# Four value products of a head group issued in one run instead of one behind each of four transposed pairs

## The reference, cut to what matters

```python
xn = _layernorm(x, axis=-1)
# attention
q, k, v = split(xn @ w_attn)                        # 16 heads of 8
scores = einsum('bhqd,bhkd->bhqk', q, k) / sqrt(8) + causal - log1p(decay * log1p(dist))
y = einsum('bhqk,bhkd->bhqd', softmax(scores), v)
attn = y @ w_proj
# experts
gate = top-2 of softmax(xn @ Wr.T), normalised
ffn = sum_e gate_e * (silu(xn @ W1_e.T) @ W2_e.T)
out = x + attn + ffn
```

## Time and profile before

| | us |
|---|---|
| median of 3 runs | 603.96 |
| lowest and highest of them | 601.05, 605.42 |
| the profiled execution, whole | 606.9 |
| its span in the trace | 604.9 |
| slots 10 to 30, first transposed pair of slot 10 to that of slot 31 | 182.80 to 418.60 |

### The profile page before, as it was taken

The page is one execution under the profiler, slowest core; times in us unless marked ns, Lnnn a source line. Parts: engine busy times, 40 slices in busy tenths (PEclk is TensorE's granted clock), DMA queues, the critical chain, the costliest instruction groups (busy, mean ns, idle before and its releaser), DMA issues.

```text
span 604.9 us, 13661 instructions
## 1 busy us (share of the span) xinstructions
PE 524.3 (87%) x4443; PEld 372.9 (62%) x4443; DVE 357.6 (59%) x1430; ACT 320.7 (53%) x576; POOL 374.5 (62%) x610
## 2 busy tenths in 40 slices
PE   3554799978889999999999999999999999999940
PEld 1443555545545655655655655655689999999930
DVE  5524588768876676676777677676333333333326
ACT  3551576646667676676676676676633333233310
POOL 3212466635669889888689879889315455545534
PEclk9999999979989999999999999999999999999975
DMA  5322359046114224314214214306425766776539
GB/s 157 131 78 71 84 176 210 2 119 174 25 62 130 82 70 124 88 68 133 64 67 140 76 61 134 97 28 209 114 73 173 219 206 200 209 211 204 154 117 317
DMA packets 69715, 76.49 MB, mean 126 GB/s; under 512 B 8318, under 2 KB 52352, under 8 KB 69648
## 3 DMA queue, kind: packets, MB, share of 16 engines
q1 hardware_dynamic: 65328, 67.16, 38.3%
q0 software_dynamic: 4320, 8.47, 4.1%
HBM read 46.16 MB, written 29.89 MB: 126 GB/s over the span
## 4 chain that ended last, share of the span: by engine, by line
PE 70%; DVE 20%; ACT 3%; DMA 2%; issue 2%; POOL 1%; SPq 0%; DVEq 0%; POOLq 0%
PE psT L1163 18%; PE psO L1175 13%; PE ps L1209 11%; PE psT L1236 11%; DVE scores L1014 10%; PE ps L1141 6%; PE psM L1118 3%; PE psM L1083 2%; PE psM L1098 2%; PE psM L1193 1%; DVE x_all L479 1%; PE psM L1124 1%; DVE y L1031 1%; DVE xn_all L845 1%; PE ps L1200 1%
## 5 line engine op out<-in xcount | busy, mean ns | idle before, releaser
L1014 DVE CUSTOM_DVE_ANT_0 scores<-ps,wdist 128x256 f32<-128x256 f32 (+3 forms) x512 | 222.0, 486 | 114.4 <-PE ps L1141 113.3
L660 POOL TENSOR_SCALAR scores<-scores,row_max 128x384 f32<-128x384 f32 (+2 forms) x448 | 224.4, 516 | 85.8 <-DVE row_max L1014 84.7
L764 ACT ACTIVATE probs<-psT 128x512 f32<-128x512 f32 x320 | 173.9, 596 | 59.6 <-PE psT L1163 59.4
L1163 PE MATMUL psT<-ident,scores 128*128 128x128 f32 x1280 | 176.3, 281 | 4.7 <-ACT probs L764 3.8
L1163 PEld LDWEIGHTS psT<-ident,scores 128*128 128x128 f32 x1280 | 140.9, 143 | 44.2 <-issue 32.2
L678 POOL DMA_INDIRECT picked_dram<-scores,row_ring x71 | 69.8, 983 | 83.8 <-DVE scores L1058 82.4
L1175 PE MATMUL psO<-probs,values 128*32 128x512 f32 (+3 forms) x1024 | 96.6, 452 | 0.0
L782 ACT ACTIVATE scores<-ps 128x512 f32<-128x512 f32 x71 | 42.4, 597 | 93.9 <-PE ps L1209 93.9
L1236 PE MATMUL psT<-wdist,scores 128*128 x568 | 75.5, 276 | 0.7 <-issue 0.4
L1209 PE MATMUL ps<-scores,wdist 128*128 128x128 f32 x568 | 75.1, 275 | 0.7 <-DVE scores L1046 0.7
L671 POOL DMA_INDIRECT rows_dram<-xn_all x64 | 62.8, 981 | 16.2 <-issue 16.2
(11 more groups left out here) (133 smaller groups left out, 356.1 us busy)
## 6 DMA issues: line engine op xcount, KB each, us to landing
wdist<-w1t SPq DMA_DIRECT2D x71, 256.0 KB, 3.3
k_rows<-k_dram SPq DMA_DIRECT2D x64, 96.0 KB, 2.9
q_rows<-q_dram SPq DMA_DIRECT2D x64, 96.0 KB, 2.5
row_ring<-rows_dram SPq DMA_DIRECT2D x71, 65.0 KB, 3.1
probs<-picked_dram SPq DMA_DIRECT2D x8, 512.0 KB, 7.3
rows_dram<-row_ring SPq DMA_DIRECT2D x7, 585.0 KB, 5.6
k_dram<-k_parts SPq DMA_DIRECT2D x8, 384.0 KB, 2.4
q_dram<-q_parts SPq DMA_DIRECT2D x8, 384.0 KB, 2.6
```

What stands on the lines that cost most here:

```text
L660: last = nc.gpsimd.tensor_scalar(part, part, -1.0, row_max[:, r, tile, quad:quad + 1], ALU.mult, ALU.add)
L764: nc.scalar.activation(probs[:, at.ring(2), w, :], psT[:, w % 2], ACT.Exp, scale=-1.0).then_inc(exp_ready, 1)
L1014: last = nc.vector.tensor_tensor_reduce(out=scores[:, r, u, col:col + n], in0=bank[:, col:col + n], in1=wdist[:, at.g * QUADS + quad, SEQ ...
L1163: last = nc.tensor.transpose(psT[:, w % 2, place * P:(place + 1) * P], scores[:, at.ring(2), u, col + key * P:col + (key + 1) * P], ident[:])
```

## The change

The three later value chunks move forward to directly behind the first. Nothing is added or removed. As ScalarE's copy of `psO` belongs to the fourth chunk, it moves with it.

```diff
     step("TE", n - 1, NGROUP, 0, 2)
     step("SA", n, NGROUP)
-    step("PV", n - 2, NGROUP, 0)
+    for chunk in range(TILES):
+        step("PV", n - 2, NGROUP, chunk)
     p1(1)
     per_batch("KR", -3)
     per_batch("QR", -2)
     step("TE", n - 1, NGROUP, 2, 4)
-    step("PV", n - 2, NGROUP, 1)
     per_batch("KM", -3)
...
     p1(2)
     step("TE", n - 1, NGROUP, 4, 6)
-    step("PV", n - 2, NGROUP, 2)
     per_batch("KL", -3)
     per_batch("QL", -2)
     p1(3)
     step("TE", n - 1, NGROUP, 6, 8)
-    step("PV", n - 2, NGROUP, 3)
     per_batch("KW", -3)
```

## The result

The changed kernel takes 633.06 us in the median (631.87 to 633.53, four runs), the kernel before 603.66 (601.05 to 605.42, four runs). The ratio is 1.049, with a 95% interval of 1.045 to 1.053: slower by 29 us, where 24 were predicted. The profiled execution took 632.73 us, 630.7 of them its span.

A forecast was written before the change was run, and what follows sets the result against it. A ring through four engines, grown by 1.29 to 12.10 us, was to set slots 10 to 30, and VectorE those before. Slot losses plus 1.5 us for the clock gave +24 on 604, so 628 us; range 616 to 641.

The forecast's parts named there:

- the ring: Loop from a slot's first pair through GpSimd's P1 steps and sends to the next; 10.81 us growing to 12.10, setting slots.
- five links: Slot 29: first pair to P1 step 1 2.02, to GpSimd 1.30, its step 1 2.00, sends 3.59, step 2 1.86 us.
- The late slots: Slots 10 to 17 and 20 to 29 at 12.10 us each: +5.7 and +8.2; slots 18 and 30 +0.8 and +1.0.
- the slack of the ring before: Slots 10 to 17 of the kernel before: mean 11.39 us against 10.81, so half a microsecond to spare, unseen.
- VectorE's chain as the second bound: Key and query slots: VectorE's P1 steps and subtractions end later, slot 12.0 to 12.1 us; holds slot 18 near 12.0.
- the early slots: VectorE's chain starts later: slots 5, 6, 7 +3.9 us; slots 2, 3, 4, 8, 9 about 0.7 each, +3.5.
- the 1.5 for the clock: New idle places drop TensorE's clock once or so, each up to 1.7 us; +1.5 us, bounds 0 and 34.
- the 1.29 of the sum: P1 step 1 stands behind 2.29 us of value products instead of 1.00; slots 5 to 7 show all 1.29.
- TensorE's own path of 11.0 us: Slots 10 to 17: 11.39 us less 0.42 saved by gathering the chunks, about 11.0 us.
- the rival of a faster kernel: TensorE's work alone counts: 30 slots gain 0.42 us each, 591 us; chance 4%.
- what would show it: Equal slots of 12.1 us; first-pair idle naming GpSimd over 15 us in slots 10 to 30; longer waits for `y` and ScalarE.
- The clock as the worst rival: TensorE's clock falls in half of the 20 slots, costing 17 us: 645 us; chance 14%.

The follow-up runs named there:

- e7: Changed kernel with only value chunks 0 and 1 in a run behind the first pair, 2 and 3 where they were before; 614.99 us, ratio 1.016.
- e12: Kernel before, chunks where they were, with four sends a slot instead of three; 617.0 us, ratio 1.020.
- e1: Changed kernel with GpSimd's sends moved from behind P1 step 1 to behind P1 step 4; 612.64 us, ratio 1.016 to the kernel before.
- e3: Changed kernel with P1 step 1 ahead of the run of four value chunks; 598.31 us, ratio 0.990 to the kernel before.
- e2: Kernel before with GpSimd's sends moved behind P1 step 4; 600.1 us, ratio 0.994.
- e6: Run of four as in the changed kernel from slot 10 on only, slots 2 to 9 as before; 623.33 us, ratio 1.033 to the kernel before.
- e4: Kernel before with chunks 0 and 1 behind the second transposed pair, 2 and 3 behind the fourth; 600.73 us, ratio 0.994.
- e9: Changed kernel with the three sends of slot 8 alone moved behind P1 step 4; 629.89 us, ratio 1.038 to the kernel before.
- e11: Changed kernel's run split: one value chunk behind each of P1 steps 1 to 4, sends last; 594.05 us, ratio 0.982 to the kernel before.

## Why the prediction was right, and where it was not

**Right: the ring and what it makes of the slots.** Four of its five links are unchanged to 0.02 us and the first grew by 1.29, as taken from the one run of four that the trace of before held. The late slots came out at 12.12 for 12.10, together +15.5 us for +15.2. e7 (half of the run inside) and e12 (another link lengthened) put the slots where the sum of the links does, and e1 (sends out of the ring) and e3 (run outside it) let them fall to the other paths.

**Misread: the slack of the ring before.** The prediction gives it half a microsecond to spare in slots 10 to 17, from their mean of 11.39 us. That mean hides the value slots, which lasted 10.81 us, the ring's own length, and 10.74 with the sends out of the ring (e2). The forecast did not suffer, as it replaced all these slots by 12.10.

**Right: VectorE's chain as the second bound,** "near 12.0". Slot 18, with two sends and hence a ring of 10.9 us, lasted 11.87, and e1's key and query slots, under no ring, lasted 11.84 and 11.87. By its own rows the chain without its gap would be 7.80 - 0.34 = 7.46 us and not "about 7.3"; the changed kernel took 7.13 in slot 14 (246.42 to 253.55).

**Mis-sized: the early slots and the clock.** The early slots were to bring 3.9 + 3.5 = 7.4 us, 8.9 with the 1.5 for the clock, and brought 11.5 between the two traces. Slots 5 to 7 gave 3.7 for 3.9, slots 2, 3, 4 and 9 gave 3.2 for 2.8, and slot 2 starts 0.7 late. The largest error is slot 8, which brought 3.8 for 0.7. The routing's instruction on VectorE, held by GpSimd, was in the trace of before, at 1.01 us for 71 columns, and I didn't ask why it was so long; the change put it where it costs 1.73. And the clock fell in that slot and again behind it. The 1.5 us for the clock had been meant for waits of slots 10 to 30, where it didn't fall in this execution; it belonged to the early ones, where it can have cost up to 4.2. The agreement in slots 5 to 7 is in part luck: they have 6.8 us at half clock in the trace of before, which the prediction doesn't mention, and some 10 in that of after. Slot 7, at full clock but for its end, grew by 1.36, which is the 1.29 of the sum; against e6 slots 5 to 7 would have grown by 6.5.

**Wrong in its kind: TensorE's own path of 11.0 us.** The 0.42 us that the run saves was subtracted in full. With nothing between them the pairs wait for ScalarE, as e3 and e4 show, and in most slots part or all of it is gone: in e3 the output slots gain 0.44, the value slots 0.25, the key and query slots nothing. It cost the forecast little, since the ring lay above that path anyway: it shows only in slots 31 and 32 (0.0 for -0.5). But in the rival of a faster kernel it weighed all. Even where nothing bounds the run, in e3, the kernel gains 1% and not the 2% of that rival (591).

**Half wrong: what would show it.** TensorE's idle time ahead of the first pair that names GpSimd was to pass 15 us in slots 10 to 30. It is 10.3 us, in seven places; only in slots of the value projection and the last three (1.33, then 1.52, 2.36 and 1.08) does it stand there. In key and query slots the slack is taken up ahead of that by `y` and by the exponentials, in output slots by TensorE's own work, and the ring closes nearly as a tie. It is the weight load of the pair that names GpSimd in all slots with sends, for 28.4 us in place of 7.2. The wait for ScalarE ahead of the fourth pair came at 0.57 for some 0.7, but TensorE waits only 0.2 us more for `y` in key and query slots, where near 1 was expected. The equal slot lengths were the better mark.

**The clock as the worst rival** did not come, with reason to keep it. The granted clock fell to 1.2 GHz behind or within idle places of 1.85, 1.84 (ahead of the step on `psM` at 162.28 in the changed kernel), 2.35 (e6), 2.51 (before, at 126.60) and 3.22 us. It did not behind 2.22, 2.36 and 2.52 (e6, at 127.34), nor behind another 1.85 in e1, ahead of its step on `psM` at 160.70.

**The changes of tiling, and the instruction that was held.** The Trainium skill, "TensorEngine Tiling (Array Packing)", section Key Properties, says that changing the tiling mode drains TensorE. The traces agree in sign: at full clock the run of four took 2.29 us again, 0.42 less than the chunks apart, with six changes fewer. For slot 8 the trace shows a VectorE instruction of 0.2 us held for 1.73 by GpSimd; the Trainium skill, "SBUF — State Buffer", section "Who interferes with whom", says that `tensor_scalar` on VectorE can use the port pair that it shares with GpSimd, and that the one that comes second blocks until the other's instruction is through. The traces agree that it is blocked and not slowed: in all but e12 it ends 0.08 to 0.12 us behind the end of a GpSimd instruction. It does not agree that the wait is for the one in progress: in the changed kernel three instructions of 256 columns ended before it got through, and the measurement decides.

## What to carry to other kernels

Where engines pass work around in order, add up the ring link by link, as its time can be the slot's while every engine looks idle in part. A block moved in front of a step lengthens every ring that the step is in, by its whole length; 2.29 us of matmuls on one side or the other of a 0.39 us step made 35 us here. And before gathering work into one run, look what its pieces covered: the best order was the opposite of a run, with the step that feeds the other engines first and a piece of the value products between every two pairs (with the sends last as well, and its early gain not explained in full). Last, compare early slots over several traces before reading a difference of 2 us: here one fall of the clock makes it.

## What the hardware did that was not expected

- An indirect DMA costs its queue on GpSimd 1.26 us each (0.96 busy, 0.30 of gap), and four instead of three add exactly that to the slots that stood at the ring's length, 10.81 to 12.07 (e12).
- A VectorE `tensor_scalar` over 71 columns took 0.19 to 1.73 us by what GpSimd did beside it. Among GpSimd's instructions of 384 and 512 columns it got through at the next end (e9: 0.21 us; e4: 0.67), among four of 256 in a row only behind the last. In e12 the one after it, a cast that takes 0.26 us in e11, took 1.95 us and ended 0.09 behind the last of the four of step 2. Why the ends within those four don't let it through stays open.
- The granted clock fell behind 2.35 us of idling in e6 and stayed up behind 2.36 in the changed kernel, at the same place of the program. At another place it fell behind 2.51 us in the kernel before and stayed up behind 2.52 in e6. What tells them apart wasn't found.
